# A graph attention kernel: 16 instead of 13 score blocks transposed by VectorE and DMA, every three pairs instead of four

## What is computed

```
h = relu(layernorm(x))
cos = beta * (h @ h.T) / (|h| |h|.T + 1e-7)
x = x + softmax(cos masked by adj, axis=1) @ h
h = relu(layernorm(x))
x = x + h @ W_self + (adj @ h / clip(rowsum(adj), 1)) @ W_neigh
```

## Time and profile before

| | |
|---|---|
| three runs, us | 480.04, 479.99, 478.88 (median 479.99) |
| profiled execution, us | 480.36 |
| its span, us | 478.6 |
| granted TensorE clock | full speed throughout (1.0) |
| busy: TensorE, VectorE, ScalarE, GpSimd | 95%, 61%, 60%, 54% |
| the 72 pairs | about 25 to 355 us |
| the aggregation after them | about 355 to 479 us |
| DMA traffic | 59.68 MB |

### The profile page before, as it was taken

How to read it: one execution, slowest core, us unless ns; L and a number is a source line. 1 busy time by engine, 2 the same in 40 slices (tenths; PEclk the granted TensorE clock), 3 DMA queues, 4 the chain that set the end, 5 groups by cost and what they waited for, 6 DMA issues and landing times.

```text
span 478.6 us, 12207 instructions
## 1 busy us (share of the span) xinstructions
PE 454.5 (95%) x5096; PEld 379.8 (79%) x5096; DVE 291.9 (61%) x685; ACT 288.3 (60%) x437; POOL 259.9 (54%) x249
## 2 busy tenths in 40 slices
PE   0869999999999999999999999999999999999997
PEld 0737888788777887788878877887787888888886
DVE  6965666877657786768857877785875321022232
ACT  2999888776976768976698779778855000000000
POOL 3989777767957568775797578667562000000000
PEclk9999999999999999999999999999999999999999
DMA  8068779888798797997799598855500000000000
GB/s 242 33 55 161 174 142 221 179 184 169 154 233 192 153 195 169 243 212 159 140 213 223 122 191 199 190 77 93 78 3 2 25 23 2 22 23 23 23 23 22
DMA packets 45899, 59.68 MB, mean 125 GB/s; under 512 B 3600, under 2 KB 38672, under 8 KB 45840
## 3 DMA queue, kind: packets, MB, share of 16 engines
q1 hardware_dynamic: 35472, 49.42, 33.4%
q0 software_dynamic: 10368, 9.44, 25.1%
HBM read 78.25 MB, written 8.91 MB: 182 GB/s over the span
## 4 chain that ended last, share of the span: by engine, by line
PE 77%; DVE 8%; ACT 8%; issue 2%; POOL 2%; DMA 1%; SPq 0%; ACTq 0%; DVEq 0%; POOLq 0%
PE ps L1185 22%; PE ps L1059 15%; PE ps L1070 7%; PE ps L1168 6%; PE ps L1165 5%; PE ps L1167 5%; PE ps L1140 5%; PE ps L1143 5%; PE ps L1142 5%; ACT word L600 3%; ACT ps L601 2%; DVE far L866 1%; DVE far L845 1%; DVE word L834 1%; DVE adj_t L689 1%
## 5 line engine op out<-in xcount | busy, mean ns | idle before, releaser
L453 POOL TENSOR_TENSOR near<-word,adj_t 128x1024 f32<-128x1024 f32 x72 | 147.3, 2046 | 82.0 <-DVE word L834 65.6
L600 ACT ACTIVATE word<-ps,small 128x512 f16<-128x512 f32 x144 | 136.3, 947 | 57.4 <-PE ps L1059 55.8
L834 DVE TENSOR_TENSOR word<-ps,word 128x512 f16<-128x512 f32 x144 | 106.2, 737 | 82.6 <-ACT ps L601 82.2
L1185 PE MATMUL ps<-table,adj_t 128*128 128x257 f16 x1024 | 115.0, 274 | 0.0
L1185 PEld LDWEIGHTS ps<-table,adj_t 128*128 128x128 fp8e4 x1024 | 100.0, 98 | 13.6
L1059 PE MATMUL ps<-unit_t 128*128 128x512 f16 x432 | 106.0, 379 | 2.8 <-DVE unit_t L732 1.7
L601 ACT ACTIVATE ps<-ps,small 128x512 f32<-128x512 f32 x144 | 108.3, 752 | 0.0
L1165 PE MATMUL ps<-table,near 128*128 128x129 f16 x576 | 102.6, 219 | 2.2 <-POOL near L453 1.5
L1168 PE MATMUL ps<-table,near 128*128 128x129 f16 x576 | 102.9, 222 | 0.0
L1167 PE MATMUL ps<-table,near 128*128 128x128 f16 x576 | 102.6, 219 | 0.0
L1140 PE MATMUL ps<-table,far 128*128 128x129 f16 x448 | 79.9, 219 | 2.6 <-DVE far L866 1.7
(11 more groups left out here) (88 smaller groups left out, 469.8 us busy)
## 6 DMA issues: line engine op xcount, KB each, us to landing
stage<-in_adj_dram SPq DMA_DIRECT2D x56, 512.0 KB, 5.5
adj_t<-in_adj_dram POOLq DMA_DIRECT2D x72, 128.0 KB, 5.0
turned_blocks<-packed SPq DMA_DIRECT2D x13, 512.0 KB, 5.4
moved_words<-turned_blocks SPq DMA_DIRECT2D x52, 128.0 KB, 4.5
x_sb<-in_x_dram SPq DMA_DIRECT2D x4, 512.0 KB, 6.3
x_again<-in_x_dram SPq DMA_DIRECT2D x7, 256.0 KB, 5.7
out_dram<-x_sb SPq DMA_DIRECT2D x7, 256.0 KB, 2.3
far<-in_x_dram SPq DMA_DIRECT2D x1, 256.0 KB, 5.1
```

Source lines behind the costliest of these rows:

```text
L453: pool.tensor_tensor(ring(near, k), ring(word, k), adj_t[:, near_adj(k)], ALU.mult).then_inc(s_near, 1)
L600: act.activation(half(word16, k, c, 0, HIGH, TPS), score(k, c), ACT.Exp, bias=exp_bias, scale=exp_scale)
L834: dve.tensor_tensor(half(word16, k, c, 0, LOW, TPS), score(k, c), half(word16, k, c, 0, HIGH, TPS), ALU.subtract).then_inc(s_elo, 1)
L1185: return pe.matmul(ps[:, agg_bank(g, t), 0:TW], adj_t[:, at:at + P], tab(b), start=(b == 0), stop=(b == T - 1))
```

## The change

`moved_pairs` takes a far pair every three instead of every four, leaves out the second and third pair of every step (`busy`), and looks for a host from k + 3 on. That gives 16 moved blocks. The DRAM buffer `turned_blocks` has one 4 KB row for each partition, so the store writes one run of 4 KB where it wrote four of 1 KB; each fetch reads the same 1 KB pieces, now from rows 4 KB apart.

```diff
--- before.py
+++ after.py
@@ -64,7 +64,7 @@
 
     x_v = x_in.rearrange("(t p) d -> p t d", p=P)
     out_v = out.rearrange("(t p) d -> p t d", p=P)
-    bounce = nc.dram_tensor("turned_blocks", [2, 4, P, ROWS // 2], fp32, kind="Internal").ap()
+    bounce = nc.dram_tensor("turned_blocks", [2, P, TILE], fp32, kind="Internal").ap()
     inv_row = nc.dram_tensor("inverse_norms", [N], fp32, kind="Internal").ap()
 
     ctx = ExitStack()
@@ -361,7 +361,7 @@
             def store_blocks(k):
 
                 sp.wait_ge(s_blocks, M_BEFORE[k] + 1)
-                sp.dma_start(bounce[M_BEFORE[k] % 2].rearrange("a p x -> p a x"), packed32[:, :].rearrange("p (a x) -> p a x", a=4)).then_inc(s_stored, 16)
+                sp.dma_start(bounce[M_BEFORE[k] % 2], packed32[:, :]).then_inc(s_stored, 16)
 
             def fetch_blocks(k):
 
@@ -369,7 +369,7 @@
                 if M_BEFORE[k] >= 1:
                     sp.wait_ge(s_far_m, M_BEFORE[k])
                 for a in range(4):
-                    sp.dma_start(slot[32 * a:32 * a + 32, :].rearrange("s (q x) -> s q x", q=4), bounce[M_BEFORE[k] % 2, a].rearrange("(q s) x -> s q x", q=4)
+                    sp.dma_start(slot[32 * a:32 * a + 32, :].rearrange("s (q x) -> s q x", q=4), bounce[M_BEFORE[k] % 2, :, 256 * a:256 * a + 256].rearrange("(q s) x -> s q x", q=4)
                                  ).then_inc(s_moved, 16)
 
             load_far(FAR[0])
@@ -1296,14 +1296,16 @@
     far = [both for _, _, both in order]
     moved, host = [], {}
     k = 8
+    began = [i for i in range(1, len(order)) if order[i][0] != order[i - 1][0]]
+    busy = [i + d for i in began for d in (1, 2)]
     while k < len(order) and order[k][0] < 5:
-        if not far[k]:
+        if not far[k] or k in busy:
             k += 1
             continue
-        at = k + 4
+        at = k + 3
+        while far[at] and (at in busy or order[at][0] >= 5):
+            at += 1
         moved.append(k)
-        if order[at][0] >= 5:
-            at = min(i for i in range(at, len(order)) if not far[i])
         host[k] = at
         k = at
     return moved, host
```

## The result

The kernel after took **482.02 us** (median of 22 runs, 479.82 to 485.26); the one before, in 22 runs beside it on the same chip, 480.05 us (478.88 to 480.81). The ratio is 1.0046 [1.0033, 1.006]: slower by 0.46%, where 478.0 was forecast and the range ended at 481.4. Of the 22 runs, 7 had a mean granted clock of 0.995 or 0.996 over the whole run (482.3 to 485.3 us). The median of the other 15 is 481.24 us, still above every run of the kernel before, so about 1.2 of the 1.97 us don't hang on the clock: by these 15 runs the ratio is 481.24 / 480.05 = 1.0025. Why 7 runs had the lower one, the traces don't show.

What follows compares the result with a forecast made beforehand. TensorE's own instruction list (busy 95% of the span) was taken as the bound. The terms, -2.64 - 1.99 + 1.26 + 0.5 + 0.9 = -1.97 us, from the 479.99 us median gave 478.0 us, range 476.0 to 481.4.

Steps and rivals of the forecast that it cites:

- Turns: On TensorE, three more moved blocks remove 3 x 8 turning transposes at 0.88 us per eight: -2.64 us.
- placement: Stalls in TensorE's slots 33, 52 and 57 lose their cause under the new plan: -0.41, -0.80, -0.78, together -1.99 us.
- the scales' waits: Near masks late behind GpSimd's second-layer scales, after short slots 19, 33 and 55: 0.42 us each, +1.26 us.
- Port: Stretch of moved-block masks with two SBUF operands, which VectorE and GpSimd instructions can shut out: +0.5 us.
- way through DRAM: Three slots instead of four between transpose and mask, so blocks fetched back from DRAM may be late: +0.9 us.
- queues: SP's three more stores and twelve more fetches ahead of far-tile loads: costed at nothing, bounds from -1.43 us.
- VectorE: Three more transposes cost nothing; three masks change kind, each stretched 0.17 us over the median: +0.5 us.
- No slack: Claim that a moved block's mask on VectorE has no slack towards TensorE, so its stretch is paid.
- The rival named for it: Each of the three added masks waits for a whole near mask (2.02 us) on GpSimd: 483.6 us, chance 0.02.
- The four short blocks: Moved blocks 19, 33, 45 and 55, with the least time through DRAM; 0.5 us late at the median store.
- The rival of starved converters: Far-tile loads stand behind fetch waits in SP's queue, so ScalarE waits: 482.3 us with three places, chance 0.13.
- 4 KB runs: The store to DRAM in 4 KB instead of 1 KB runs: no gain, 0; at most 2.4 us per store.

Runs made afterwards that it cites:

- e5: Kernel before with the moved blocks' mask taking its words from PSUM instead of SBUF: 479.34 us, ratio 0.9985.
- e11: Kernel after with the moved blocks' mask reading PSUM and all far-tile loads but the first two at a quarter of their bytes: 476.6 us, ratio 0.9931.
- e14: Kernel after with all far-tile loads but the first two at a quarter of their bytes, masks still reading SBUF: 480.62 us, ratio 1.0019.
- e4: Kernel after with the moved blocks' mask reading VectorE's own transposed block, not waiting for the fetch; stores and fetches still made: 481.24 us, ratio 1.0031.
- e1: Kernel after with the old form of the store, four runs of 1 KB per partition: 481.5 us, ratio 1.0027.
- e2: Kernel before with the new 4 KB form of the store, old plan kept: 479.59 us, ratio 1.0002.
- e17: Kernel before with the moved blocks' mask reading PSUM and short far-tile loads (a quarter of the bytes): 478.38 us, ratio 0.9963.

## Why the prediction was wrong

The sum had two parts, and both came out otherwise. Turns, placement and the scales' waits, -3.37 us, are what the plan brings by itself: measured -1.8. Port, way through DRAM and queues, +1.4 us, are what it pays: measured, new plan against old, +2.7 to +3.7 (worked out below).

**Turns, -2.64: right.** 24 instructions fewer, and the slot account closes with it.

**Placement, -1.99: right but for 0.2** in the three slots that it named. Slots 33, 52 and 57 gave back 0.41, 0.80 and 0.58; of the last, 0.39 was the port's (e5). The waits for the scales in slots 20, 34 and 56 cost 0.16 each, 0.49 for all (e11), where I had 1.26: too dear. What the step left out stands below as the missing term.

**The plan by itself, -3.37: half of it.** 478.38 - 476.6 = 1.8 us in favour of the new plan with port and queues taken out. That this is close to the -1.97 forecast for all is luck: the forecast's figure holds +0.5 for the port, which neither of these two kernels pays, and +0.9 for lateness on the way through DRAM, which wasn't there.

**VectorE, +0.5: the step that failed.** I took the mean stretch of the old masks, 0.17 us, and charged it for the three added ones. Two things were wrong in that. A mean over masks isn't a price: a stretched mask costs nothing where it has slack (slot 28) and its whole stretch where it has none. And the plan moves the other masks too, onto the seventh pairs, where the word chunk comes late; that all sixteen had to be laid beside GpSimd's timeline at their new places I didn't see. The port costs the new plan 1.4 to 2.4 us with full loads (1.0025 or 1.0046 less 0.9996) and 4.0 with light ones (e14 against e11), where the old plan pays 0.7. "No slack" was also wrong as a rule for all: in the profiled execution of the kernel before, the moved masks of slots 16, 29 and 49 were done 0.5 to 0.7 us ahead of TensorE. The rival named for it, 483.6 us at a chance of 0.02, had the mechanism and not the places: I let the three added masks each meet a near mask, and what they met was mostly the 1.06 us conversion, at the four seventh pairs.

**A term that was missing, +1.9.** Beside the stretch, those four slots lose 0.58, 0.58, 0.20 and 0.55 us even in e11, 1.9 us in all, against 0.08 in the old slot 22 and nothing in the other three: "every other instruction stays" was true of TensorE and said nothing of when VectorE gets its words. That was hidden in the placement step, which looked for stalls that go and at only one kind that comes.

**The way through DRAM, +0.9: not there.** One fetch of sixteen was late, by 0.26 us. In slot 25 that let a near mask go first and so cost up to 2.2 us in this execution, a price of the port again; e4 shows no gain in the median without the wait. The four short blocks, for which the step feared, waited for no fetch.

**The queues, 0: under-priced.** They cost the new plan between 0.3 us (1.0025 - 1.0019, with the port; 1.3 from 1.0046) and 3.1 (0.9996 - 0.9931, without it), and the old one 0.22% (0.9985 - 0.9963, without the port), 1.1 us. I had seen the one stall of slots 24 and 25 and asked whether it stays; and I had put all of it, 1.43 us, down to the load, when the 0.83 of slot 25 was for the most part a stretched mask. In the profiled execution of the kernel after there are four waits for a load, as before, 6.1 us in all for 8.4, but spread over slots 22, 25, 58 and 61, so a single execution doesn't show the price; taking the loads' bytes away did. The rival of starved converters had given 482.3 us, close to the measured time for a reason that is only part of it.

**4 KB runs, 0: right** in time, e1 and e2. The store's median did fall, which I hadn't expected.

Together, port and queues take 5.5 us from the new plan (1.0046 - 0.9931; 4.5 from 1.0025) and 1.8 (1 - 0.9963) from the old one, 3.7 us more (2.7). Less the 1.5 that the plan brings by ratios, that is the 2.2 us (1.2) of the ratio. This is the same numbers added up and no check by itself; the slots are one. Their losses are 6.09 us in e11 and 5.24 in e17, so port and queues cost 10.57 - 6.09 = 4.5 us in the new plan (after, e11) and 7.13 - 5.24 = 1.9 in the old one (before, e17), 2.6 more, and less 1.8 that is the 0.8 us by which the span grew. The 0.8 us between 482.02 and 481.24 come with the seven runs at the lower clock, and what brings those is open.

## What to carry to other kernels

When a plan moves work between slots, draw up for every moved instruction when its input is ready, when its reader wants it, and what runs beside it on an engine that it shares a port with; the average stretch of its kind over the old places says nothing of the new ones. A saving on the bounding engine is real only at places where its feeders are in time: twelve well-placed blocks beat sixteen. Take two suspected causes out together as well as singly, since one (starved converters) can hide the other (the port). And compare a clean pair of kernels with the terms that it can pay, not with the whole forecast.

## What the runs showed of the hardware that was not expected

- The mask with two SBUF operands doesn't slow down beside a GpSimd instruction that was first, it waits for its end and then runs at full speed: ends 1.08 and 1.09 us after it, where the mask alone takes 1.21. It goes both ways (a conversion of 1.77 for 1.06). With one operand from PSUM it is never over 1246 ns in the rows shown.
- The bytes of the far-tile loads set the scatter: 3.0 us between the fastest and the slowest of the full-clock runs with full loads, 0.4 with a quarter of the bytes.
- A store in one 4 KB run per partition lands in 4.6 us at the median, in four 1 KB runs in 5.4, both beside the loads of the old plan.
- Seven of 22 runs of the kernel after had a mean clock of 0.995 or 0.996. Of the twelve of e1, the same plan, one had it (481.9 us); of the runs of the kernel before beside the experiments (478.8 to 482.6 us in the comparisons), none. What brings it is open.
